# Layer norm of the deep experts: tokens turned onto the partitions, statistics by batch statistics from PSUM, turned back; gates by one product

## The reference

```
t = t + ffn(_ln_t(t))                      # t: tokens, 64 channels each; _ln_t: eps 1e-5
L0, L2:  logits = xf @ Wg + bg             # 8 experts, top 2, softmax over the two
         out = sum_e w[:, e] * (gelu(xf @ W1[e] + b1[e]) @ W2[e] + b2[e])
L3:      xn = (xt - mu) * rsqrt(var + 1e-5)   # a second norm of the already normed token
         experts read xn * ln_g[e] + ln_b[e]; the router reads xt itself
```

## Time and profile before

| stretch (us from the span's start) | us | PE busy | DVE busy | ACT busy | POOL busy | granted PE clock |
|---|---|---|---|---|---|---|
| whole span | 1914.4 | 1705.4 (89%) | 915.8 | 912.6 | 521.6 | 0.95 |
| deep experts L0, 133 to 420 | 287.0 | 278.67 | 127.40 | 152.78 | 71.58 | 0.99 |
| deep experts L2, 1203 to 1488 | 285.0 | 277.18 | 128.16 | 152.24 | 71.58 | 1.00 |
| `layer_norm_twice` for L3, 1622 to 1655 | 33.0 | 18.63 | 9.77 | 24.10 | 0.00 | 0.76 |
| deep experts L3, 1655 to 1914.4 | 259.4 | 250.47 | 94.84 | 141.80 | 71.05 | 0.98 |

### The profile page before, as it was taken

One profiled execution on the slowest core, in us unless ns is written; L12 is line 12 of the kernel. 1 busy time (PEld: TensorE's weight loads), 2 busy tenths in 40 slices (PEclk: granted clock), 3 DMA queues, 4 the chain that ended last, 5 costly groups with the idle time before them and its releaser, 6 DMA issues. The chain is left out here.

```text
span 1914.4 us, 51089 instructions
## 1 busy us (share of the span) xinstructions
PE 1705.4 (89%) x21120; PEld 788.8 (41%) x21120; DVE 915.8 (48%) x1920; ACT 912.6 (48%) x1210; POOL 521.6 (27%) x692
## 2 busy tenths in 40 slices
PE   7989999998998899789888877999999587699998
PEld 3543444433333333233777762444443232233333
DVE  3544444534665556430566654444543277243433
ACT  3225555554555344444444436355555500655554
POOL 0001222220000254501566652022222055032223
PEclk8999999998999899899899988999999898799999
DMA  5003223220000566057234411223232030134242
GB/s 241 12 11 71 64 46 89 45 45 34 12 1 23 132 147 144 18 202 289 77 100 133 138 42 69 45 56 79 45 89 46 5 37 3 41 93 112 73 112 61
DMA packets 64242, 147.46 MB, mean 77 GB/s; under 512 B 35512, under 2 KB 35640, under 8 KB 59920
## 3 DMA queue, kind: packets, MB, share of 16 engines
q1 hardware_dynamic: 64144, 146.22, 28.4%
HBM read 106.07 MB, written 25.44 MB: 69 GB/s over the span
## 5 line engine op out<-in xcount | busy, mean ns | idle before, releaser
L1295 ACT ACTIVATE ARENA<-PS,W 128x1024 f32<-128x1024 f32 x384 | 406.6, 1111 | 248.3 <-PE PS L1228 164.8
L1127 POOL TENSOR_TENSOR ARENA<-ARENA 128x512 f32<-128x512 f32 x168 | 214.2, 1275 | 786.7 <-DVE ARENA L1417 786.1
L1200 PE MATMUL PS<-ARENA,W 64*128 64x512 f32 x1536 | 358.3, 606 | 3.4 <-DVE ARENA L1348 3.4
L1228 PE MATMUL PS<-ARENA,W 128*64 128x512 f32 x1536 | 350.8, 599 | 2.6 <-DVE ARENA L1417 2.6
L1417 DVE SCALAR_TENSOR_TENSOR ARENA<-PS,W,ARENA 128x512 f32<-128x512 f32 x192 | 143.3, 750 | 325.7 <-PE PS L1228 304.8
L1200 PEld LDWEIGHTS PS<-ARENA,W 64*128 64x128 f32 x1536 | 141.0, 187 | 205.4 <-issue 104.5
L1228 PEld LDWEIGHTS PS<-ARENA,W 128*64 128x64 f32 x1536 | 101.8, 136 | 214.6 <-issue 206.5
L635 POOL TENSOR_TENSOR ARENA<-ARENA 128x512 f32<-128x512 f32 x56 | 71.0, 1268 | 296.3 <-DVE ARENA L969 294.7
L2346 PE MATMUL PS<-ARENA 32*32 32x32 f32 x8448 | 103.2, 197 | 5.7 <-issue 5.4
L807 ACT ACTIVATE ARENA<-PS,W 128x1024 f32<-128x1024 f32 x64 | 67.9, 1111 | 68.8 <-PE PS L711 68.8
L2346 PEld LDWEIGHTS PS<-ARENA 32*32 32x32 f32 x8448 | 93.4, 106 | 8.6 <-issue 6.1
(11 more groups left out here) (249 smaller groups left out, 2352.6 us busy)
## 6 DMA issues: line engine op xcount, KB each, us to landing
ARENA<-scratch_g SPq DMA_DIRECT2D x64, 768.0 KB, 9.6
ARENA<-scratch_g SPq DMA_DIRECT2D x64, 256.0 KB, 3.9
W<-w_dram SPq DMA_DIRECT2D x1, 7307.5 KB, 25.1
ARENA<-XN SPq DMA_DIRECT2D x12, 512.0 KB, 3.8
ARENA<-XN SPq DMA_DIRECT2D x24, 256.0 KB, 2.5
scratch_x<-ARENA SPq DMA_DIRECT2D x8, 512.0 KB, 3.9
scratch_b<-ARENA SPq DMA_DIRECT2D x8, 512.0 KB, 4.1
scratch_z<-ARENA SPq DMA_DIRECT2D x8, 512.0 KB, 3.9
```

The costliest lines, as they stand in the source:

```text
L1127: nc.gpsimd.tensor_tensor(SUM[:, k, :], SUM[:, k, :], TMP[:, e % 2, :], ALU.add)\
L1200: last = mm(PS[:, (u % UPS) * R + r, :], w(layer + "_w1", b * 128, (b + 1) * 128, half(r)), XS[half(r), t % 2, :], start=True, stop=True)
L1228: last = mm(PS[half(r), out_of(e), :], w(layer + "_w2", b * C, (b + 1) * C), H[:, u % HS, r * T:(r + 1) * T], start=part == 0, stop=part = ...
L1295: f(H[:, u % HS, :], PS[:, at:at + R, :].rearrange("p a b -> p (a b)"), ACT.Gelu, bias=w(layer + "_b1", b, b + 1)).then_inc(e_gelu.sem, 1)
```

## The change

In all three deep stages the norm is done with tokens on the partitions. `turn_in` transposes the 512 columns of the next tile (four transposes) into the bank that `center` had. VectorE's `measure` takes batch statistics of 64 columns of that bank eight times; `invert` joins the two halves of each statistic (six steps), adds eps, takes the Newton steps and then, still from the bank, subtracts the mean and multiplies by the inverse root in eight instructions of 64 columns. `turn_back` transposes the result (four transposes) into the other bank, ScalarE's `copy` moves it into XS, and the router scores come from XS. For L3 the same is done with a second eps (`renorm`): the experts read the twice normed token and the scores are multiplied by a ratio; `layer_norm_twice` and the DMAs of the input go. The gates are turned by one product with 64 columns of weights instead of four with 16, copied as 64 rows of 128, and written and read in pieces of a group (WB is laid out group by group). The order of banks becomes in, 0, 1, back, 2, 3, logits, 4, 5, turn, 6, 7, and the hand-written places change.

```diff
@@ deep_experts: schedule, the same for L0, L2 and L3
+            NEWTON = 6 + KINDS + 2 + 3 * 3 + 2 * (KINDS - 1)
-                order = ["center", 0, 1, "logits", 2, 3, "scale", 4, 5, "turn", 6, 7]
-                pe_at = {0: "center", 0.5: "logits", 2: "scale", 3: "turn"}
-                act_at = {(0, 1): "square", (1, 1): "widen", (2, 1): "bend", (3, 1): "rows"}
-                dve_at = {-1: "keep", 1: "invert", 3: "rank norm", 4: "weigh"}
+            order = ["in", 0, 1, "back", 2, 3, "logits", 4, 5, "turn", 6, 7]
+            after_scale = {0: 0, 2: 2, 4: 4, 6: 6, "in": -1, "back": 1, "logits": 3, "turn": 5}
+            at_last = {3: 1, 5: 3, 7: 5}
+            pe_at = {0: "in", 1: "back", 1.5: "logits", 3: "turn"}
+            act_at = {(1, 3): "copy", (2, 3): "bend", (3, 2): "rows"}
+            dve_at = {-1: "measure", 0: "invert", 3: "rank", 4: "weigh"}
@@ spread
-                        sp.dma_start(gates[p].rearrange("r e t -> (r e) t"), RT[0:GW, k, :])\
+                        sp.dma_start(gates[p].rearrange("g r (e t) -> (g r e) t", e=E), RT[0:G * GW, k, 0:TOK])\
...
-                                sp.dma_start(WB[half(r), k, lo:hi, :],
-                                             gates[p, r:r + 1, lo:hi, :].to_broadcast([C, hi - lo, T]))\
+                                sp.dma_start(WB[half(r), k, :, lo * TOK:hi * TOK],
+                                             gates[p:p + 1, :, r, lo * TOK:hi * TOK]
+                                             .to_broadcast([C, G, (hi - lo) * TOK]))\
@@ TensorE
+                    def turn_in(p):
+                        behind("in", p - 1)
+                        for g in range(G):
+                            last = nc.tensor.transpose(PS[:, out_of("in"), g * TOK:(g + 1) * TOK],
+                                                       X[:, p * T + g * TOK:p * T + (g + 1) * TOK], w("ident"))
+                        last.then_inc(ln_centered.sem, 1)
+
+                    def turn_back(p):
+                        behind("back", p - 1)
+                        pe.wait_ge(ln_scaled.sem, ln_scaled.at(p + 1))
+                        for g in range(G):
+                            last = nc.tensor.transpose(PS[:, out_of("back"), g * TOK:(g + 1) * TOK],
+                                                       CEN[:, g * TOK:(g + 1) * TOK], w("ident"))
+                        last.then_inc(ln_varied.sem, 1)
@@ transpose (the gates)
-                        for g in range(G):
-                            last = mm(PS[0:GW, out_of("turn"), g * TOK:(g + 1) * TOK], GATES[:, g, :], w("ident"),
-                                      start=True, stop=True)
-                        last.then_inc(g_turned.sem, 1)
+                        mm(PS[0:G * GW, out_of("turn"), 0:TOK], GATE.rearrange("p a e -> p (a e)"), w("ident"),
+                           start=True, stop=True).then_inc(g_turned.sem, 1)
@@ emptied
-                        elif norms and e == 1:
-                            pe.wait_ge(ln_taken.sem, ln_taken.at((t + 1) * 2 + 1))
-                        elif norms and e == 5:
+                        elif e == 1:
+                            pe.wait_ge(ln_scaled.sem, ln_scaled.at(t + 2))
+                        elif e == 3:
                             pe.wait_ge(ln_normed.sem, ln_normed.at(t + 2))
@@ entry: fill after each of the three first steps
-                        if norms and pe_at[n] != "turn":
-                            fill(UPS * R - 1, 1 + (pe_at[n] == "logits"))
+                        if pe_at[n] != "turn":
+                            fill(UPS * R - 1, 2)
@@ ScalarE
-                    def square(p):
...
-                    def widen(p):
...
+                    def copy(p):
+
+                        act.wait_ge(ln_varied.sem, ln_varied.at(p + 1))
+                        nc.scalar.copy(XS[:, p % 2, :], PS[:, out_of("back"), :]).then_inc(ln_normed.sem, 1)
@@ VectorE
+                    def measure(p):
                         dve.wait_ge(ln_centered.sem, ln_centered.at(p + 1))
-                        v.tensor_copy(CEN, PS[:, out_of("center"), :]).then_inc(ln_taken.sem, 1)
+                        for n in range(GR):
+                            last = v.bn_stats(STATS[:, n, :], PS[:, out_of("in"), n * C:(n + 1) * C])
+                        last.then_inc(ln_squared.sem, 1)
 
                     def invert(p):
+                        dve.wait_ge(ln_squared.sem, ln_squared.at(p + 1))
+                        step(v.tensor_tensor(APART, STATS[:, :, 1], STATS[:, :, 4], ALU.subtract))
...
+                        for n in range(GR):
+                            last = v.tensor_scalar(CEN[:, n * C:(n + 1) * C], PS[:, out_of("in"), n * C:(n + 1) * C],
+                                                   MEAN[:, n:n + 1], EXPERT_INV[:, n:n + 1], ALU.subtract, ALU.mult)
+                        last.then_inc(ln_scaled.sem, 1)
+                        if renorm:
+                            step(v.tensor_tensor(RATIO, VAR[:, GR:], EXPERT_INV, ALU.mult))
+                            step(v.tensor_tensor(RATIO, RATIO, INV[:, 0:GR], ALU.mult))
@@ calls
-        once = ARENA[:, ROUTED]
-        layer_norm_twice(once, XN, X)
-        deep_experts("L3", norms=0, router=once,
+        deep_experts("L3", renorm=True,
```

More of the change, by code:

```diff
@@ L161, in take @@
                 return ap
-        ROUTED = slice(ARENA_N - Q * S, ARENA_N)
         loaded = count("loaded")
@@ L1007, in experts, with deep_experts @@
             g_chain.base += ROUTES * (RANK + WEIGH)
-        def deep_experts(layer, norms=1, router=None, out=None):
+        def deep_experts(layer, renorm=False, out=None):
             blocks = HIDDEN[layer]
             NB = E * blocks
-            NORMS = norms
-            assert blocks == 2 and norms < 2
+            assert blocks == 2
             G = T // TOK
@@ L1142, in behind @@
                             pe.wait_ge(e_scaled.sem, e_scaled.at(count))
-                    def center(p):
-                        behind("center", p - 1)
-                        mm(PS[:, out_of("center"), :], w("center"), tile(X, p),
-                           start=True, stop=True).then_inc(ln_centered.sem, 1)
+                    def turn_in(p):
[4 more added lines that the diff above has]
+                        last.then_inc(ln_centered.sem, 1)
@@ L1167, in scale @@
-                    def scale(p):
-                        behind("scale", p - 1)
-                        pe.wait_ge(ln_log.sem, ln_log.at(p + 1))
-                        for g in range(G):
-                            last = mm(PS[:, out_of("scale"), g * TOK:(g + 1) * TOK],
-                                      WIDE[:, g, :], w("ident"), start=True, stop=True)
-                        last.then_inc(ln_scaled.sem, 1)
                     def transpose(p):
@@ L1177, in transpose @@
                         pe.wait_ge(g_split.sem, g_split.at(p + 1))
-                        for g in range(G):
-                            last = mm(PS[0:GW, out_of("turn"), g * TOK:(g + 1) * TOK], GATES[:, g, :], w("ident"),
-                                      start=True, stop=True)
-                        last.then_inc(g_turned.sem, 1)
+                        mm(PS[0:G * GW, out_of("turn"), 0:TOK], GATE.rearrange("p a e -> p (a e)"), w("ident"),
+                           start=True, stop=True).then_inc(g_turned.sem, 1)
                     def prepare(what, p):
-                        if what == "center":
-                            center(p)
-                        elif what == "scale":
-                            scale(p)
+                        if what == "in":
+                            turn_in(p)
+                        elif what == "back":
+                            turn_back(p)
                         elif what == "logits":
@@ L1331, in invert @@
                                              ALU.mult, ALU.add))
-                        for _ in range(3):
+                        for n in range(3):
                             step(v.tensor_tensor(NEWT, INV, INV, ALU.mult))
@@ L1391, in run @@
                             for what in steps.split():
-                                if what == "keep":
-                                    keep(p)
+                                if what == "measure":
+                                    measure(p)
+                                elif what == "invert":
+                                    invert(p)
                                 elif what == "rank":
@@ L1397, in run @@
                                     weigh(p)
-                                elif what == "invert":
-                                    invert(p)
-                                    take(p)
-                                elif what == "norm":
-                                    norm(p, k)
                         return run
@@ L1434, in _ @@
                     tile_of(NT - 1, 1, NT // 2 - 1, more=False)
-            if not norms:
-                for c in e_input:
```

(1 more changed line is left out.)

183 lines of the change are left out of this document (45 added, 138 removed).

## The result

The changed kernel takes 2210.32 us, the median of four runs (2206.89 to 2215.58), against 1927.03 us before: 1.147 times as long, with a 95% interval of 1.1442 to 1.1499. The prediction was slower, 2173 us, in a range of 2080 to 2250. Direction and mechanism held; the size was 37 us short, and under that sum lie larger errors with opposite signs.

The account below looks back on a forecast made before the run. TensorE was taken as full. Waits and clock of 13.5 us a tile, with TensorE's work, gave 162 us in L0 and L2 and 104 in L3; entries -20: 246 on 1927, so 2173 us, range 2080 to 2250.

Parts of the forecast that it names:

- TensorE is the bound and a wait in it is paid in full: L0 tile: TensorE busy for all of its 33.87 us, so added work or a wait there is paid in full.
- Rival 1: Three banks free when TensorE comes to them, so only its work counts: 1888 us; chance 4 in 100.
- rival 2: TensorE waits only at expert 1, since ScalarE's copies don't come behind held GELUs: 2064 us; chance 8 in 100.
- Wait at expert 1: Before expert 1's products, TensorE waits for VectorE's last scaling: 6.3 us a tile, 6.6 in L3.
- costed at nothing: Gates' DMAs in smaller pieces add no time; pieces landing 2 us later would add about 1 at expert 1.
- The scalings' pitch: In `invert`, eight scalings of 64 columns from PSUM, 0.21 us apart, 1.7 in all.
- Waits at experts 3 and 7: TensorE waits for ScalarE's copy and row copy, each behind a held GELU: 3.0 and 1.7 us a tile.
- The clock: Half-speed work after waits: 2.0 us after expert 1 and 0.5 after expert 3, together 2.5 a tile.
- between 1.0 and 4.3: Bounds in us for a tile's clock loss: clock often holds, or both slow stretches always occur.
- rival 3: Clock stays low after each wait: 5 us lost a tile gives 2226 us, ten 2330; chance 10 in 100.
- TensorE's own work: Preparing steps: 5.0 us removed, 3.1 added, saving 1.9 a tile in L0 and L2; 1.1 more in L3.
- Entries: Starts of the three stages: 2 us more each in L0 and L2, 24 less in L3; together 20 less.

## Why the prediction held, and where it was off

**TensorE is the bound and a wait in it is paid in full: right.** Waits at three places, each for the helper named, 21 times each, 252 us in the trace for 233 predicted. With all three taken away the time is that of before (1929.97). Rival 1 (TensorE not held) and rival 2 (only expert 1 waits) are refuted by the waits themselves.

**Wait at expert 1: 6.3 predicted, 7.27 in a steady tile, 7.8 on the mean.** By the terms in VectorE's rows: the start of the weighing 0.74 later than assumed, the scalings 2.11 in place of 1.7, TensorE ready 0.15 later; the chain was right (3.65 for 3.6). The first term is the step that failed: the gate DMAs were costed at nothing, with the remark that a landing 2 us later would cost about 1. The pieces are smaller, the packets of an execution went from 64242 to 81522 (61940 with the old gates and the new norm), and the landing came late enough to cost 0.74 us here; with the old gates the steady tile's wait is 6.52. At the first tiles of the stages it was worse, 10.4 to 11.6 us of wait. The scalings' pitch was taken from 128 columns of another form, 0.21; 64 columns with two column operands took 0.25 from one to the next (eight of them, the last one taking 0.335, make 2.11), inside the upper bound of 0.29.

The Trainium skill, "VectorE: DVE Perf Modes", section on the TRN2 errata, advises, for instructions that read SBUF, tiles of at least 512 elements because each instruction pays a fixed latency. The trace agrees in kind: in the version with the early turn in, one copy of the whole bank takes 0.68 us (at 194.06), and eight scalings of an eighth of it, there from SBUF, 1.87 (at 201.91), though these are two different operations. By the figure that the Trainium skill gives there, 64 columns from PSUM take an estimated 0.19 us; the 0.25 measured is above it.

**Waits at experts 3 and 7: right.** 2.75 for 3.0 and 1.43 for 1.7. Expert 3's products began, behind ScalarE's copy, 4.69 us after expert 2's, for 4.8; TensorE came 0.15 later than the 1.79 assumed, since half of a `down` batch takes 1.94 until it is through. The row copy is 0.25 us for 0.35.

**The clock: 2.5 a tile predicted, 3.9 measured. This is the main error, and its place is the wait at expert 3.** In the windows from each wait to TensorE's next one, half clock costs 41.5 us after the 21 waits at expert 1, 2.0 a tile and exactly the forecast's term, 41.3 after those at expert 3, again 2.0 a tile where I took 0.5, and nothing after those at expert 7. Removing the wait at expert 3 gave the same 2.0 beside the wait itself. It comes in 12 of the 21 tiles; the same 74 records after this wait, in a tile with the low clock and in one without:

```profile
233.67:252.80 19.13, 19.13 (x74) 0.82 0.01 1
427.44:443.30 15.86, 15.86 (x74) 1.00 0.00 1
```

The nearest row, TensorE after 3.04 us, has 3.30 us at 0.50 and so 1.65. The prediction called its wait just as long as that one and took 0.5 without giving another reason; that step failed. The total lies just inside the step "between 1.0 and 4.3", and rival 3, with 5 us a tile and 2226 us, was a little nearer to it than the forecast. With the 12 us that aren't clock the products and scores grew by 95 / 21 = 4.5 a tile, and for those 12 the forecast had no term.

The Trainium skill, "TensorE: Matmul & The Clock Gate", section "HAM oscillation — how this bites in real kernels", describes a loop whose every round waits, throttles and begins again at half clock, and advises to gather the work so that the engine waits less often. The trace agrees: with the waits 795.5 us of products, without them 721.4.

**TensorE's own work: 19 us less predicted, 35 measured.** The step that failed is the reading of the earlier trace rows. I called a group of eight records there four transposes; linear attention turns eight blocks of 128 columns, one record each. A plain fp32 product of 128 columns is two records (eight for the four of the old gate turn, 0.98 us, 0.245 each); a transpose is one (0.58 us for the four at 228.40, 0.145 each; by the earlier trace rows 0.93 for eight, 0.116). So two groups cost 1.2 us and not 1.9, the saving in L0 and L2 is 2.6 a tile (1.9 predicted), and the sentence in the prediction that transposes take as long as plain products is wrong. The rule of the Trainium skill that it weighed ("four times faster", an estimated 0.5 us for both groups) is too low by as much as my row was too high: by the trace a transpose takes about half of a plain product.

**Entries: -20 predicted, -15 measured.** L3 as forecast (the first weighing comes 30.2 us after the first product, 29 predicted). L0 and L2 lose 4.0 and 3.2 us until the first `up` in place of 2.

So the errors were +30 at expert 1, -11 at experts 3 and 7, +43 for the unchanged products and scores (31 of it the clock), -16 for the work and +5 at the entries: +51, against 48 between the forecast and the spans. That the total came out within 2% owes something to opposite signs.

**Open.** Which wait at expert 3 is followed by a low clock isn't settled. All are 2.75 us or, a few, 3.03; in the changed kernel 12 of 21 are followed by it. With `invert` ahead of the weighing, and with one Newton round, where the wait at expert 1 is 5.3 and 6.5 us on the mean in place of 7.8, it is 2 of 21 each, though every wait at expert 1 there is still followed by a low clock. For example, with `invert` first the window after the 2.75 (230.92 to 237.42) has 1.00, though a wait of 5.36 and 8.29 us at 0.65 went ahead. With the bank copy, where TensorE doesn't wait for the scalings at expert 1 at all, it is 13 of 21. This suggests that a second wait's price depends on what went ahead of it; the runs show what each wait costs on the mean, not a rule for the single one.

## What to carry to other kernels

When an in-order engine is full, ask of every helper result not how long it takes but which bank it holds until then, and who stands in line for that bank; a chain of small instructions belongs where its bank isn't waited for, and one copy of the bank to SBUF (0.7 us here) freed 145 us. Price a wait on TensorE with what comes behind it: here 252 us of waiting cost another 95 us in unchanged products, 83 of it at half clock, and a step of 0.2 us in the chain cost about 0.4. And count what a record is (one instruction or half of one) in the code before a duration is taken from a grouped row.

## What the hardware showed that I had not expected

- A transpose of 128 x 128 fp32 is one record, and a group of eight or four is followed 0.93 or 0.58 us later by the next, 0.116 to 0.145 each; a plain fp32 product of 128 columns is two records, 0.245 together.
- Eight batch statistics over 64 PSUM columns take 1.15 us, 0.13 from one to the next; eight scalings of 64 columns with two column operands take 2.11 from PSUM, 0.25 apart, and 1.87 from SBUF.
- A wait of 2.75 us was followed by 9.77 us at 0.65 in one tile and by a clock of 1.00 in others, 12 and 9 of 21 in the changed kernel; the wait's own length doesn't tell which. With one Newton round, where the wait ahead of it is 1.3 us shorter on the mean, it was 2 of 21.
- Putting products without use into the waits gained 60 us on the chip, with the waits as long as before.
- Spreading the same bytes in smaller pieces, with the norm unchanged, raised the packets from 61940 to 81522 and the median landing of a 256 KB spread from 3.9 to 5.4 us.
